# A token mixture of experts on one Trainium2 core: token number and gates carried as four more columns of each scattered row

## The reference

```
x = hidden.reshape(-1, 512)                      # 2048 tokens
probs = softmax(x @ w_router.T)                  # 8 experts
expert_weight, expert_idx = top_k(probs, 2)
expert_weight = expert_weight / sum(expert_weight)
for each token and each of its 2 experts e:
    out_e = square(relu(x @ w1[e].T)) @ w2[e].T
    moe_out[token] += weight * out_e
shared_out = square(relu(x @ ws1.T)) @ ws2.T
return shared_out + moe_out                      # added to the residual x
```

## Time and profile before

| | |
|---|---|
| time, median of 3 runs | 1307.7 us (1301.9 to 1309.49) |
| the profiled execution | 1305.85 us |
| its span in the trace | 1304.0 us |
| mean granted TensorE clock | 0.986 |
| busy: PE, PEld, DVE, ACT, POOL | 1252.7, 865.2, 754.2, 376.2, 232.0 us |
| DMA | 358.27 MB in 106664 packets, mean 275 GB/s |
| chain that ended last, by engine | PE 79%, DMA 9%, DVE 4%, issue 4% |

### The profile page before, as it was taken

One profiled execution on the slowest core, in us unless ns is written; L12 is line 12 of the kernel. 1 busy time (PEld: TensorE's weight loads), 2 busy tenths in 40 slices (PEclk: granted clock), 3 DMA queues, 4 the chain that ended last, 5 costly groups with the idle time before them and its releaser, 6 DMA issues.

```text
span 1304.0 us, 22845 instructions
## 1 busy us (share of the span) xinstructions
PE 1252.7 (96%) x7814; PEld 865.2 (66%) x7815; DVE 754.2 (58%) x1400; ACT 376.2 (29%) x613; POOL 232.0 (18%) x203
## 2 busy tenths in 40 slices
PE   6999999999999999998999999999984999999997
PEld 3444444444444444467888888899963988887885
DVE  4546556555445545479888778666441345555554
ACT  2312212121111211326555544433211222322322
POOL 1000000000000000003222226405364002222222
PEclk9999999999999999999999999999995999999999
DMA  9999999999999999706777787904550477776765
GB/s 354 411 418 415 415 416 417 419 419 418 419 419 410 403 395 391 298 1 239 266 266 270 281 293 266 222 28 153 198 197 1 108 261 178 167 183 148 183 152 91
DMA packets 106664, 358.27 MB, mean 275 GB/s; under 512 B 20848, under 2 KB 41328, under 8 KB 92016
## 3 DMA queue, kind: packets, MB, share of 16 engines
q1 hardware_dynamic: 97408, 338.94, 69.4%
q0 software_dynamic: 9200, 18.65, 7.5%
HBM read 352.76 MB, written 67.71 MB: 322 GB/s over the span
## 4 chain that ended last, share of the span: by engine, by line
PE 79%; DMA 9%; DVE 4%; issue 4%; SPq 1%; ACT 1%; POOL 0%; ACTq 0%; DVEq 0%; POOLq 0%
PE ps L1982 14%; PE ps L1870 13%; PE ps L2054 11%; PE ps L2044 10%; DMA parts_low<-split 5%; PE ps L2342 5%; PE ps L2336 5%; PE ps L2339 4%; PE ps L1945 4%; PE ps L1828 3%; PE ps L1960 2%; DMA arena<-ctx_n 2%; DMA high<-parts_low 1%; PE ps L1920 1%; PE ps L1927 1%
## 5 line engine op out<-in xcount | busy, mean ns | idle before, releaser
L2054 PE MATMUL ps<-split 128*128 128x256 f32 x1536 | 197.6, 287 | 7.5 <-issue 4.0
L2054 PEld LDWEIGHTS ps<-split 128*128 128x128 f32 x1536 | 190.3, 194 | 13.3 <-issue 12.0
L1982 PE MATMUL ps<-arena 128*64 128x512 f32 (+1 forms) x832 | 192.3, 594 | 0.0
L1870 PE MATMUL ps<-arena 128*64 128x512 f32 (+1 forms) x1024 | 178.6, 505 | 2.0 <-DVE arena L1135 1.2
L1870 PEld LDWEIGHTS ps<-arena 128*64 128x64 f32 x1024 | 65.5, 137 | 122.5 <-issue 119.9
L1982 PEld LDWEIGHTS ps<-arena 128*64 128x64 f32 (+1 forms) x832 | 58.3, 137 | 112.4 <-issue 111.7
L1231 DVE SCALAR_TENSOR_TENSOR arena<-arena,hbar 128x512 f32<-128x512 f32 x128 | 90.5, 749 | 67.9 <-PE ps L1945 66.3
L767 ACT ACTIVATE arena<-ps 128x512 f32<-128x512 f32 (+1 forms) x93 | 52.2, 580 | 242.2 <-PE ps L1945 180.3
L2044 PE MATMUL ps<-split_ws,split 128*128 128x512 f32 x360 | 90.4, 400 | 17.6 <-issue 17.0
L653 POOL TENSOR_TENSOR arena<-arena,row_b 128x512 f32 (+1 forms) x16 | 20.2, 1268 | 474.1 <-DVE arena L1105 446.4
L757 POOL DMA_INDIRECT out<-arena,token_i x39 | 60.6, 1554 | 236.8 <-DVE arena L1799 135.0
(11 more groups left out here) (235 smaller groups left out, 2003.8 us busy)
## 6 DMA issues: line engine op xcount, KB each, us to landing
arena<-ctx_t SPq DMA_DIRECT2D x122, 800.5 KB, 17.9
high<-parts_low SPq DMA_DIRECT2D x78, 1024.0 KB
arena<-ctx_n SPq DMA_DIRECT2D x96, 768.0 KB, 14.4
arena<-ctx_n SPq DMA_DIRECT2D x32, 1024.0 KB, 15.8
parts_high<-split SPq DMA_DIRECT2D x16, 1024.0 KB, 8.7
parts_low<-split SPq DMA_DIRECT2D x16, 1024.0 KB, 10.0
moe_in<-zero SPq DMA_DIRECT2D x3, 3328.0 KB
stage_raw<-w1t SPq DMA_DIRECT2D x8, 1024.0 KB, 6.6
```

The costliest lines, as they stand in the source:

```text
L1870: last = mm(bank(n)[S * h:S * (h + 1), 0:w], qT[:, k, S * h:S * (h + 1)], ctxT[h][:, k, at_j:at_j + w], start=(k == 0), stop=(k == KD - 1))
L1982: last = mm(bank(7)[S * h:S * (h + 1), :], ET[0:w, c, S * h:S * (h + 1)], ctxN[h][0:w, c, :], start=(c == 0), stop=(c == JC - 1))
L2054: last = mm(dst[:, 2 * P * m:2 * P * (m + 1)], w[a][:, k, c], tokens[b][:, k, :], start=(k + i == 0), stop=(k == KD - 1 and i == 2))
```

## The change

Four more columns travel with each row. `moe_in` gets rows of DI = D + 4 floats (2064 bytes), `slot_info` is gone, and the two `hs` buffers are 516 wide and stand at `ZERO_AT + D`. The four columns are: token number, first gate, second gate, first slot. DVE copies them from `info` (now a view of `stats`) behind the normed row of each tile, and the same 32 indirect DMAs carry them; the 32 small ones go. A slot can tell which of the two gates is its own by comparing the first slot with its own number (`own_slot`, an iota into `causal_b`, which nobody reads by then): four small DVE operations after `of_slot` is read.

With it: SP's fill goes to the columns of `moe_in` (16 bytes a row) and `of_slot` is read from them; the spare rows of `out` are zeroed by four indirect DMAs of POOL early in stage b in place of one of SP; each of POOL's scatters waits for the fill too; POOL's iota of the token numbers waits for the last variances; DVE's router waits at tile 2 for all stored parts, since `hs` now stands in the third raw buffer; and `load_low1(0)` stands behind the scatters, because its place overlaps `hs`.

```
--- before.py
+++ after.py
@@ -47,6 +47,7 @@
 NS = 2 * E
 NB = 3
 NY = 4
+DI = D + 4
 ZEROED = 3
 TY = (TX + T) // 2
 TA = T
@@ -60,8 +61,7 @@
 
 def perceiver_layer(nc, x, ctx_n, ctx_t, w1, w23, b_sim, w_qv, b_qv, wq, wk, wv, wm, b_qk, bv, bm,
                     w_router, w1t, w2t, ws1t, ws2t, out):
-    moe_in = nc.dram_tensor("moe_in", [GT * P, D], F32).ap()
-    slot_info = nc.dram_tensor("slot_info", [GT * P, 2], F32).ap()
+    moe_in = nc.dram_tensor("moe_in", [GT * P, DI], F32).ap()
     parts_high, parts_low = ([nc.dram_tensor(f"{n}{i}", [E * P, KD * D], F32).ap() for i in range(2)]
                              for n in ("parts_high", "parts_low"))
 
@@ -96,9 +96,11 @@
         hbar = sb("hbar", [P, 2, KD, 2])
         rinv = sb("rinv", [P, H])
         rmax = sb("rmax", [P, H])
-        info = [sb(f"info{k}", [P, T, 2]) for k in range(2)]
-        of_slot = sb("of_slot", [P, GT, 2])
-        no_token = sb("no_token", [P, NY, 2])
+        info = stats[:, :, 0:DI - D]
+        of_slot = sb("of_slot", [P, GT, DI - D])
+        no_token = sb("no_token", [P, NY, DI - D])
+        own_slot = causal_b[:, 0:GT]
+        spare_i = sb("spare_i", [P, NY], I32)
         cdot, smax, nsmax, smx, erow, rs = (small[:, i:i + 1] for i in range(6))
         bmax, nbmax, bsum, brec = (per_batch[:, i, :] for i in range(4))
 
@@ -249,10 +251,10 @@
 
         at(0)
         assert TH * D == 2 * KD * D
-        at(2 * KD * D)
-        hs = [carve(D) for _ in range(2)]
-        carve(2, D)
-        assert used[0] == 3 * KD * D, used[0]
+        at(ZERO_AT + D)
+        hs_rows = [carve(DI) for _ in range(2)]
+        hs = [h[:, 0:D] for h in hs_rows]
+        at(3 * KD * D)
         at_pr = used[0]
         pr, pr2, eq, cand, oh0, oh1, msk, tot, inc0, inc1 = (carve(T, E) for _ in range(10))
         inc = [inc0, inc1]
@@ -337,7 +339,7 @@
         rows_in = sem("rows_in")
         w1_in, w2_in, wr_in = (sem(n) for n in ("w1_in", "w2_in", "wr_in"))
         pool_filled = sem("pool_filled")
-        CONSTS, KBD0, VBD0, KBD1, VBD1, ZERO, NOTOKEN, IOTA = 9, 10, 13, 14, 17, 18, 20, 27
+        CONSTS, KBD0, VBD0, KBD1, VBD1, ZERO, NOTOKEN, SPARE, IOTA = 9, 10, 13, 14, 17, 18, 20, 22, 28
         raw_in, high_done, low_done, low_pool, parts_out = (
             [sem(f"raw_in{i}") for i in range(NB)], sem("high_done"), sem("low_done"), sem("low_pool"), sem("parts_out"))
         hold = sem("hold")
@@ -394,8 +396,8 @@
                              "y_done", "y_ready"))
         y_out = [sem(f"y_out{i}") for i in range(NY)]
         low2_back = sem("low2_back")
-        info_filled, info_ready, info_out, info_in, token_ready = (
-            sem(n) for n in ("info_filled", "info_ready", "info_out", "info_in", "token_ready"))
+        info_filled, info_ready, info_in, token_ready = (
+            sem(n) for n in ("info_filled", "info_ready", "info_in", "token_ready"))
 
         def xg_of(g):
 
@@ -481,7 +483,7 @@
 
             def zero_slots(q):
                 n = GT // ZEROED
-                dst = moe_in.rearrange("(g p) d -> p g d", p=P)[:, n * q:n * (q + 1), :]
+                dst = moe_in.rearrange("(g p) d -> p g d", p=P)[:, n * q:n * (q + 1), 0:D]
                 sp.dma_start(dst, zero[:, :].unsqueeze(1).to_broadcast([P, n, D])).then_inc(slots_zeroed, 16)
 
             for n in range(NS):
@@ -507,12 +509,10 @@
             for q in range(1, ZEROED):
                 zero_slots(q)
             sp.wait_ge(pool_filled, NOTOKEN)
-            info_v = slot_info.rearrange("(g p) c -> p g c", p=P)
+            info_v = moe_in.rearrange("(g p) c -> p g c", p=P)[:, :, D:DI]
             for i in range(NY):
                 to = info_v[:, i:GT:NY, :]
-                sp.dma_start(to, no_token[:, i:i + 1, :].to_broadcast([P, to.shape[1], 2])).then_inc(info_filled, 16)
-            sp.dma_start(out[T * P:(T + NY) * P, :].rearrange("(i p) d -> p i d", p=P),
-                         zero[:, :].unsqueeze(1).to_broadcast([P, NY, D])).then_inc(x3_out, 16)
+                sp.dma_start(to, no_token[:, i:i + 1, :].to_broadcast([P, to.shape[1], DI - D])).then_inc(info_filled, 16)
             sp.wait_ge(out_done, T)
             high_v = [h.rearrange("(e p) n -> p e n", p=P) for h in parts_high]
 
@@ -531,7 +531,7 @@
 
             sp.wait_ge(x3_ready, TH // 2)
             store_rows(slice(0, TH // 2))
-            sp.wait_ge(x3_out, 32)
+            sp.wait_ge(x3_out, 16)
             load_w2(ARENA, 6, 7)
             sp.wait_ge(h2lo_ready, 6)
             load_w1(2, 3)
@@ -565,8 +565,7 @@
                 load_low(g, parts_low[1], LOW2, low2_back)
 
             read_group(0)
-            load_low1(0)
-            sp.wait_ge(x3_out, 48)
+            sp.wait_ge(x3_out, 32)
             load_w2(ARENA + KD * D, 7, 8)
             sp.wait_ge(token_ready, NY)
             load_w2(3 * KD * D, 3, 4)
@@ -577,6 +576,7 @@
             store_rows(slice(TH, TR))
             for i in range(2):
                 sp.wait_ge(scat[i], 32 * (T // 2))
+            load_low1(0)
 
             def load_slots(g):
 
@@ -588,9 +588,6 @@
                                  ).then_inc(xg_in, 16)
 
             load_slots(0)
-            sp.wait_ge(info_out, 16 * (2 * T - NY))
-            for i in range(NY):
-                sp.wait_ge(y_out[i], 16)
             sp.dma_start(of_slot[:, :, :], info_v).then_inc(info_in, 16)
             sp.wait_ge(sh_done, 4 * (TA // 2))
             load_w1(0, 1)
@@ -621,7 +618,7 @@
                     if g > 0:
                         sp.wait_ge(y_done, g)
                     load_low2(g + 1)
-            sp.wait_ge(x3_out, 16 * 5)
+            sp.wait_ge(x3_out, 16 * 4)
 
 
         @block.gpsimd
@@ -675,7 +672,16 @@
             nc.gpsimd.memset(zero[:, :], 0.0).then_inc(pool_filled, 1)
             nc.gpsimd.iota(no_token[:, :, 0], pattern=[[P, NY]], base=T * P, channel_multiplier=1,
                            allow_small_or_imprecise_dtypes=True).then_inc(pool_filled, 1)
-            nc.gpsimd.memset(no_token[:, :, 1], 0.0).then_inc(pool_filled, 1)
+            nc.gpsimd.memset(no_token[:, :, 1:], 0.0).then_inc(pool_filled, 1)
+            nc.gpsimd.iota(spare_i[:, :], pattern=[[P, NY]], base=T * P, channel_multiplier=1).then_inc(pool_filled, 1)
+            pool.wait_ge(dve_step, 1)
+            nc.gpsimd.iota(own_slot, pattern=[[P, GT]], base=0, channel_multiplier=1,
+                           allow_small_or_imprecise_dtypes=True).then_inc(pool_filled, 1)
+            pool.wait_ge(pool_filled, SPARE)
+            for i in range(NY):
+                nc.gpsimd.indirect_dma_start(
+                    out, bass.IndirectOffsetOnAxis(ap=spare_i[:, i:i + 1], axis=0), zero[:, :], None
+                ).then_inc(y_out[i], 16)
             pool.wait_ge(rows_in, 64)
 
             def add_bm(t):
@@ -722,32 +728,24 @@
                            allow_small_or_imprecise_dtypes=True).then_inc(pool_filled, 1)
             nc.gpsimd.iota(iota_ny, pattern=[[NY, GT // NY + 1]], base=0, channel_multiplier=0,
                            allow_small_or_imprecise_dtypes=True).then_inc(pool_filled, 1)
-            for k in range(2):
-                nc.gpsimd.iota(info[k][:, :, 0], pattern=[[P, T]], base=0, channel_multiplier=1,
-                               allow_small_or_imprecise_dtypes=True).then_inc(pool_filled, 1)
+            pool.wait_ge(var_ready, 9)
+            nc.gpsimd.iota(info[:, :, 0], pattern=[[P, T]], base=0, channel_multiplier=1,
+                           allow_small_or_imprecise_dtypes=True).then_inc(pool_filled, 1)
 
             with pool.Fori(0, T // 2) as n:
                 for i in range(2):
                     pool.wait_ge(hs_ready, 2 * n + i + 1)
-                    pool.wait_ge(idx_ready, 4 * n + 2 * i + 2)
+                    pool.wait_ge(idx_ready, 6 * n + 3 * i + 3)
                     pool.wait_ge(slots_zeroed, 16 * ZEROED)
+                    pool.wait_ge(info_filled, 16 * NY)
                     pool.sem_inc(hold, 1)
                     for k in range(2):
                         nc.gpsimd.indirect_dma_start(
-                            moe_in, bass.IndirectOffsetOnAxis(ap=idx[k][i][:, :], axis=0), hs[i], None
+                            moe_in, bass.IndirectOffsetOnAxis(ap=idx[k][i][:, :], axis=0), hs_rows[i], None
                         ).then_inc(scat[i], 16)
 
-            pool.wait_ge(info_ready, 2)
-            pool.wait_ge(pool_filled, IOTA)
-            pool.wait_ge(info_filled, 16 * NY)
-            for t in range(T):
-                for k in range(2):
-                    nc.gpsimd.indirect_dma_start(
-                        slot_info, bass.IndirectOffsetOnAxis(ap=slot_i[k][:, t:t + 1], axis=0), info[k][:, t, :], None
-                    ).then_inc(info_out if 2 * (T - t) > NY else y_out[2 * (t - T) + k + NY], 16)
-
             pool.wait_ge(token_ready, 1 + NY)
-            pool.wait_ge(x3_out, 16 * 5)
+            pool.wait_ge(x3_out, 16 * 4)
             for g in range(GT):
```

(16 more changed lines are left out.)

48 lines of the change are left out of this document (23 added, 25 removed).

## The result

| | before | after |
|---|---|---|
| time, median | 1308.6 us (1301.9 to 1312.46, 4 runs) | 1277.68 us (1277.34 to 1279.89, 4 runs) |
| the profiled execution, its span | 1305.85, 1304.0 us | 1277.49, 1275.8 us |
| mean granted TensorE clock | 0.986 | 0.998 |

The ratio is 0.9765, 95% interval 0.9738 to 0.9793: faster, by 31 us. That was measured on one chip; on another, in the experiments, the same change gains nothing that can be measured.

What follows compares the result with a forecast made beforehand. It took a PE stall of 32.3 us beside POOL's 32 8-byte scatters as the removable loss. Stall -32.3 and slot loads +1.0 gave -31.3 on 1305.85, or 1276 us against the 1307.7 median; range 1270 to 1286.

Steps and rivals of the forecast that it cites:

- the stall: PE's gaps in the shared expert's loop during POOL's 32 small scatters; removing them was to save all 32.3 us.
- expert loop, slot loads: Expert loop's loads of 512-byte pieces no longer start on multiples of 512; +1.0 us over 39 groups, from 0 to 4.
- stage b, with POOL's scatters of zeros: Four scatters of zeros ahead of POOL's additions at 589.80 take 5.1 us on POOL, costing 0 overall.
- `load_low1(0)`, DVE's copies, `of_slot`, waits: The moved load, 2.9 us of copies, operations after the slot read, and added waits were all to cost 0.
- 0 on the path: The zeros delay POOL's additions, but DVE first waits for one at 619.93, 24 us after they ended: no cost.
- the clock follows: In the shared loop the granted TensorE clock halves only after PE was already running single matmuls with gaps.
- What is left is POOL's scatter with an 8-byte element.: With other candidates excluded, POOL's 8-byte scatters into `slot_info`, 958.6 to 1001.0 us, were blamed for the 32.3 us loss.
- scatters as such are harmless: The 32 whole-row scatters between 886.5 and 957.2 us lie beside passes in which PE is never idle.
- (A): Rival, chance 0.09: shared-loop gaps come from PE's own instruction supply, not the scatters; change worth +1 us, about 1309.
- (B): Rival, chance 0.07: 2064-byte rows are cut, so the stall moves to the wide scatters from 886.5; 53 us more, 1329.
- (C): Rival, chance 0.02: slot loads bound the expert loop; past the slack each further us costs 38 us, 1314 at one.

Runs made afterwards that it cites:

- e6: Changed kernel with POOL's four scatters of zeros moved behind the first four additions of stage b; 1276.06 us on chip R, ratio 0.9994 to the kernel before.
- e13: The kernel of e6 unchanged, run on chip S beside the changed kernel; 1276.15 us, ratio 0.9997 to the kernel before.
- e4: Changed kernel with 32 scatters of 64 bytes a row into an unused tensor, where the small ones stood; 1309.04 us on chip Q.
- e14: Changed kernel with 32 scatters of 512 bytes a row added where the small ones stood, on chip T; 1309.05 us, ratio 1.0031 to the kernel before.
- e3: Changed kernel with 16 scatters of 8 bytes a row into an unused tensor, where the small ones stood; 1289.98 us on chip Q.
- e1: Kernel before with four scatters of 512 bytes a row into an unread tensor replacing its 32 small ones; 1271.24 us on chip Q, ratio 0.9758.
- e10: Changed kernel with one 8-byte scatter added behind each of the 32 wide ones, on the same semaphores; 1296.01 us on chip R.
- e9: Changed kernel with 32 scatters of 8 bytes a row added in stage a, ahead of POOL's first work of stage b; 1279.61 us on chip R.
- e2: Changed kernel with 32 scatters of 8 bytes a row into an unused tensor, where the small ones stood; 1307.84 us on chip Q.
- e5: Changed kernel with 32 scatters of 512 bytes a row into an unused tensor, where the small ones stood; 1279.35 us on chip R.

## Why the prediction was right, and where it was not

**The time.** 1276 against 1277.68, inside 1270 to 1286. By terms, predicted and measured:

| term | predicted | measured |
|---|---|---|
| the stall | -32.3 | -32.3 |
| expert loop, slot loads | +1.0 (0 to 4) | +1.4 on P, -0.2 on S: not resolved |
| stage b, with POOL's scatters of zeros | 0 | +2.6 at the stall's start |
| `load_low1(0)`, DVE's copies, `of_slot`, waits | 0 | hidden |

The forecast lies 1.7 us from the median, nearer than its terms deserve. Between the two profiled executions the difference is 28.4 us and not 31.3, and the 2.6 us of stage b, which the forecast had at nothing, are most of what is missing. They show at the first expert matmuls, which came at 1019.87 where about 1017 was forecast; that the medians lie 30.9 us apart is luck.

**The term that was missed** is "0 on the path" for the scatters of zeros. The prediction looked for who waits for POOL's additions, found DVE at 619.93 with 24 us in hand, and was right on that. It didn't look at what DVE was doing beside them. Moving POOL's 5.99 us from 589.80 to 595.44 laid it over DVE's chain of 128x2 operations, which is on PE's path. By e6 and e13 that accounts for PE's delay at 610 us; the time that they win there is lost again by 850, so how much of the 2.6 us at the stall's start is the zeros' stays open. The kernel before had a sign of it, in its timeline of DVE:

```profile
592.59 2.07 DVE L1416 TENSOR_TENSOR arena<-arena,rmax 128x1024 f32<-128x1024 f32 x1
...
602.47 1.23 DVE L1416 TENSOR_TENSOR arena<-arena,rmax 128x1024 f32<-128x1024 f32 x1
```

The first of these lies within POOL's additions and takes 0.84 us more than the second, which doesn't.

**The stall** was read rightly in what it costs, what goes on beside it and that the clock follows. The clock has its share all the same: the gaps in the trace of the kernel before sum to 21.6 us, and the other 10.7 of the 32.3 are matmuls that took longer, in the stretch from about 974 to 1008 us, where the granted clock is at half. The cause went one step too far: "What is left is POOL's scatter with an 8-byte element." e4 and e14 refute the 8 bytes. The step that failed is "scatters as such are harmless", drawn from the 32 wide ones: POOL's timelines have them by fours, with pauses of 1.2 us and more between, while 28 of the small ones came without a pause right behind the last four wide ones, and the last four after 3 us. Such a run is not harmful from its start: in e3 it is 20 long, from 958.6 to 984.8 us, and the first gap is at 975.5. So the change works because it takes a run of scatters away, not because it makes rows wide, and e1 shows that no other part of the change was needed for the gain. That a run without pauses is what counts fits all of this, but no kernel here spread the scatters out on a chip that stalls (e10 fell on chip R), so it isn't shown. Nor is it known whether the stall needs this loop of PE's, as e9 fell on R as well.

**The rivals.** (A) fell by e1, e2 and e3, which move the end of the gaps by moving the end of the scatters. It left a true remainder: what PE lacks in the gaps is put down to no engine, and why isn't settled. A fetch of instructions that the profile records isn't it: in the kernel before no packet of the instruction queues starts between 966 and 1004 us. (B) didn't happen: PE is busy 22.42 of 22.42 us in the passes with the wide scatters of 2064 bytes. (C) didn't either: DVE's waits for slots from 1040 us on are 15.5 and 15.4 us in 10 each with a longest of 1.6, where before they were 13 each with the same longest.

**What the prediction had no case for** is the chip. P, Q and T take 1304 to 1309 us for the kernel before, R and S 1276 to 1277; the change is worth 31 us on P and, by its ratio, nothing on S. On S the trace of the kernel before shows the stall absent; on R none was taken, but e5's shows it absent from a program that stalls on T. What differs between the chips stays open: an expectation of "faster" rested on one chip's runs.

## What to carry to other kernels

Before an operation of POOL is moved in time, look not only for who waits for its result but for what DVE does in the new place: a two-input operation of 0.16 us was held for 3.5 us. Check the end of the stage too, since moving it away again won 2.8 us at 610 and nothing by 850. Where PE shows "issue" gaps within a straight run of matmuls, look for a long run of POOL's indirect DMAs beside them (rows of 8 to 512 bytes did the same), and compare a second chip before a gain of that kind is counted on. Putting the data into scatters that are there anyway gained 31 us on P and cost nothing that the runs resolve on S, the two chips on which the changed kernel itself was timed.

## What the runs showed of the hardware

- A run of 32 indirect DMAs of POOL, most of them 1.26 us after the one before, takes 29.7 to 32.3 us from PE on P, Q and T and none on R and S; 16 take 10.5 us on Q. Nobody needs to wait for them, and rows of 8, 64 and 512 bytes do the same.
- In such a stall PE gets one to a few matmuls at a time, with gaps of 0.2 to 2.4 us between (19 to 23 gaps in the four traces with 32); the granted clock falls to half (1.2 GHz) only after the gaps have begun, and is full again in the slice after the stall.
- DVE's operation on two SBUF inputs of 128x2, started inside POOL's additions, took 3.54 and 3.53 us in the two traces of the changed kernel, 3.53 in five of its variants, and 0.16 with the additions moved away.
- Rows of 2064 bytes, and pieces of 512 bytes read from them, cost nothing that the traces resolve over 39 groups: 237.8 and 234.3 us with them, 236.4 and 234.5 with rows of 2048.
